# Hand-fetched quarter groups twice as often: a graph layer's row gathers on SyncE and ScalarE

## The reference

```python
h = jnp.maximum(_layernorm(x, axis=-1), 0.0)
cat = jnp.concatenate((h[src], h[dst], edge_attr_128), axis=-1)      # 200000 x 384
msg = jax.nn.relu(cat @ W1 + b1)
aggr = jax.ops.segment_sum(msg, dst, num_segments=12500)
return x + gamma * layernorm(aggr + h) + beta
```

## Time and profile before

| | |
|---|---|
| median of three runs | 2796.62 us (2792.42 to 2845.8) |
| span of the profiled execution, first to last instruction | 1949.5 us |
| the profiled execution's own time | not among the times shown |
| TensorE's mean granted clock | 0.899 |
| HBM read, written | 281.72 MB, 23.64 MB |
| one-row issues of SP and of ACT | 1024 and 1024 |
| POOL's gathers from `table_a` | 1484 |

### The profile page before, as it was taken

How to read it: one execution, slowest core, us unless ns; L and a number is a source line. 1 busy time by engine, 2 the same in 40 slices (tenths; PEclk the granted TensorE clock), 3 DMA queues, 4 the chain that set the end, 5 groups by cost and what they waited for, 6 DMA issues and landing times.

```text
span 1949.5 us, 52908 instructions
## 1 busy us (share of the span) xinstructions
PE 1548.5 (79%) x11881; PEld 1483.7 (76%) x11881; DVE 1256.9 (64%) x3454; ACT 659.4 (34%) x1507; POOL 1463.9 (75%) x1559
## 2 busy tenths in 40 slices
PE   5688788778878787877787788787788888877887
PEld 5678788777777777877777787777777877777786
DVE  7656666667666666666666676666566665656665
ACT  5533333333333333333333333333323232322323
POOL 7777777777777777777777777777777777777776
PEclk9888888989889998998989998999898888888988
DMA  9755656556565655656565565656556565555554
GB/s 261 204 143 144 167 143 166 152 156 166 144 169 145 164 152 155 163 147 169 149 160 153 155 166 144 168 140 168 147 154 163 138 164 148 155 148 153 163 145 106
DMA packets 229468, 306.84 MB, mean 157 GB/s; under 512 B 46461, under 2 KB 141157, under 8 KB 229317
## 3 DMA queue, kind: packets, MB, share of 16 engines
q1 hardware_dynamic: 151858, 192.55, 34.4%
q0 software_dynamic: 49536, 101.55, 21.4%
q10 hardware_dynamic: 27922, 11.43, 2.7%
HBM read 281.72 MB, written 23.64 MB: 157 GB/s over the span
## 4 chain that ended last, share of the span: by engine, by line
issue 22%; DMA 22%; POOL 20%; PE 13%; DVE 10%; DVEq 8%; ACT 2%; ACTq 2%; POOLq 1%; SPq 0%
DMA a_rows<-table_a,picks 20%; POOL a_rows L613 19%; DVEq L1398 5%; DVE onehot_cols L1367 3%; PE ps_pre L769 3%; PE ps_pre L770 3%; PE ps_sum L781 2%; DVE msg L1387 2%; PE ps_edge L756 2%; PE ps_fin L781 1%; DVE aggr L1408 1%; ACTq L1027 1%; DMA table_a<-a_out 1%; DVEq L1383 1%; PE ps_sum L788 1%
## 5 line engine op out<-in xcount | busy, mean ns | idle before, releaser
L613 POOL DMA_INDIRECT a_rows<-table_a,picks x1484 | 1401.8, 945 | 452.4 <-issue 400.3
L769 PE MATMUL ps_pre<-w_c,edge_cols 128*128 128x128 f32 x3128 | 671.5, 300 | 29.5 <-issue 29.2
L770 PE MATMUL ps_pre<-b_win,onehot_cols 128*128 128x128 f32 x3128 | 663.2, 297 | 0.0
L995 ACT ACTIVATE msg<-msg 128x512 f32<-128x512 f32 x390 | 245.7, 630 | 951.9 <-DVE msg L1387 893.1
L769 PEld LDWEIGHTS ps_pre<-w_c,edge_cols 128*128 128x128 f32 x3128 | 537.1, 215 | 38.6 <-issue 37.0
L1387 DVE TENSOR_TENSOR msg<-ps_pre,a_rows 128x512 f32<-128x512 f32 x374 | 257.0, 687 | 433.8 <-DMA a_rows<-table_a,picks 339.4
L770 PEld LDWEIGHTS ps_pre<-b_win,onehot_cols 128*128 128x128 f32 x3128 | 534.7, 214 | 0.0
L1367 DVE SCALAR_TENSOR_TENSOR onehot_cols<-space,base_all,ps_hot 64x512 f32<-64x512 int32 x391 | 438.3, 1121 | 0.6 <-DMA space<-in_dst 0.6
L781 PE MATMUL ps_sum<-onehot,msg 128*128 128x64 f32 x1560 | 214.6, 283 | 105.2 <-ACT e_rows L1013 71.3
L781 PEld LDWEIGHTS ps_sum<-onehot,msg 128*128 128x128 f32 x1560 | 200.5, 201 | 123.4 <-ACT e_rows L1013 82.2
L991 ACT ACTIVATE edge_cols<-ps_edge 128x512 f32<-128x512 f32 x391 | 228.4, 584 | 136.8 <-PE ps_edge L756 115.7
(11 more groups left out here) (137 smaller groups left out, 1073.8 us busy)
## 6 DMA issues: line engine op xcount, KB each, us to landing
edges<-in_edge_attr SPq DMA_DIRECT2D x195, 512.0 KB
space<-in_dst SPq DMA_DIRECT2D x195, 256.0 KB
a_rows<-table_a,picks POOLq DMA_INDIRECT x1484
hand_rows<-table_a SPq DMA_DIRECT2D x1024, 0.5 KB
hand_rows<-table_a ACTq DMA_DIRECT2D x1024, 0.5 KB
b_win<-table_b SPq DMA_DIRECT2D x391, 32.0 KB
table_b<-b_rows ACTq DMA_DIRECT2D x96, 64.0 KB
out<-out_rows SPq DMA_DIRECT2D x96, 64.0 KB
```

Of the source, the lines that this page charges most:

```text
L613: pool.indirect_dma_start(a_rows[:, u, k, :], None, table_a[:, :], bass.IndirectOffsetOnAxis(ap=picks[:, u, k:k + 1], axis=0),).then_inc(s ...
L769: pe.matmul(to, edge_cols[:, u % 2, k * P:(k + 1) * P], w_c[:, :], start=True, stop=False)
L770: mm = pe.matmul(to, onehot_cols[:, u % 2, k * P:(k + 1) * P], b_win[:, u, :], start=False, stop=True)
L995: act.activation(msg[:, u % 2, :, :], msg[:, u % 2, :, :], ACT.Relu).then_inc(s_msg, 1)
```

## The change

PERIOD goes from 6 to 3: a quarter group in each third round is fetched by hand, 32 lists (HANDS) for 16, so POOL gathers three quarters for group 0 in each third round. Of each list's 128 rows SP now issues 80 (ten batches of eight), ACT 48 (twelve slots of four). In a turn of three rounds SP sends a batch after each window of the first two (four a round) and after the first two windows of the third; ACT sends a slot in each group of all three. The lists run one round ahead of their use: the round of use is the first of the turn for the next list. In the first two rounds SP's ten batches are packed closer and ACT sends eights. `hand_rows` gets a second buffer (each with its semaphore), used in turn, and a list waits for the use of the list two before. `hand_picks` is laid out in places of 16 numbers (64 bytes) of which the first eight are used. The loops of POOL, ACT and DVE are cut at the rounds with a hand-fetched quarter; SP's loop still has six rounds a turn, its last turn stands outside the loop.

```diff
-PERIOD = 6
+PERIOD = 3
 BATCH = 8
+PLACE = 16
-ACT_ROWS = 64
+ACT_ROWS = 48
...
-        hand_picks = sb("hand_picks", [HANDS, P], I32)
-        hand_rows = sb("hand_rows", [P, 1, H])
+        hand_picks = sb("hand_picks", [HANDS, P // BATCH, PLACE], I32)
+        hand_rows = sb("hand_rows", [P, 2, H])
...
         def hand_numbers(t, first, n):
+            batch, at = first // BATCH, first % BATCH
             if isinstance(t, int):
-                return hand_picks[t:t + 1, first:first + n]
-            return bass.at_runtime_partition(hand_picks[0:1, first:first + n], t)
+                return hand_picks[t:t + 1, batch, at:at + n]
+            return bass.at_runtime_partition(hand_picks[0:1, batch, at:at + n], t)
+
+        def hand_slots(s, j):
+            t = s * 2 + (0 if j < 2 else 1 if j < EARLY - 1 else 2)
+            third = j + 1 if j < 2 else j - 2 if j < EARLY - 1 else 0
+            return t, (j + 1) // PERIOD % 2, third
+
+        def hands_used(t):
+            return ((t - 2) * PERIOD + PERIOD - 1) * UNROLL + 1
...
                 def fetch(t, par, batch):
-                    if batch == 0 and past(t, 1):
-                        sp.wait_ge(s_z, ((t - 1) * PERIOD + PERIOD - 1) * UNROLL + 1)
+                    if batch == 0 and past(t, 2):
+                        sp.wait_ge(s_z, hands_used(t))
                         sp.sem_inc(s_gate_sp, 1)
                     numbers = numbers_of(mybir.EngineType.SP, t, batch * BATCH, BATCH)
-                    for n in range(BATCH):
-                        sp.dma_start(hand_row(batch * BATCH + n, par), row_at(numbers[n])
+                    for p in range(BATCH):
+                        sp.dma_start(hand_row(batch * BATCH + p, par), row_at(numbers[p])
                                      ).then_inc(s_hand_rows[par], 16)
...
                         window(i, u, base[u])
-                        if t is not None and (j, u) in SP_SLOTS:
-                            fetch(t, par, SP_SLOTS.index((j, u)))
+                        if hands is not None:
+                            t, par, batches = hands
+                            for batch in batches[u]:
+                                fetch(t, par, batch)
...
-                SP_SLOTS = [(j, u) for j in range(1, PERIOD - 1) for u in (1, 3)]
+                SP_BATCHES = [[[0], [1], [2], [3]], [[4], [5], [6], [7]], [[8], [9], [], []]]
+                SP_FIRST = [[[0], [1], [2], [3]], [[4], [5, 6], [7], [8, 9]]]
...
+                def hand_round(i, groups):
+                    for u in range(groups):
+                        step(i, u, HAND_K if u == 0 else SUB)
...
-                        if t is not None and j * UNROLL + u < len(ACT_SLOTS) and ACT_SLOTS[j * UNROLL + u]:
-                            fetch(t, par, j * UNROLL + u)
+                        if hands is not None:
+                            t, par, first, n = hands
+                            if first + u * n < ACT_ROWS:
+                                fetch(t, par, first + u * n, n)
...
-                ACT_SLOTS = [0] * UNROLL + [4] * (ACT_ROWS // 4)
+                SLOT, FIRST_SLOT = BATCH // 2, BATCH
...
-            dve.tensor_scalar(hand_picks[:, :], hand_ids[:, :, HAND_K], float(ROW_BYTES), None, ALU.mult
-                              ).then_inc(s_hand_picks, 1)
+            dve.tensor_scalar(hand_picks[:, :, 0:BATCH],
+                              hand_ids[:, :, HAND_K].rearrange("t (b e) -> t b e", e=BATCH), float(ROW_BYTES), None,
+                              ALU.mult).then_inc(s_hand_picks, 1)
...
-                        dve.wait_ge(s_hand_rows[0], handed * (P * 16))
-                        dve.tensor_tensor(msg[:, u % 2, HAND_K, :], ps_pre[u % 2][:, HAND_K * H:], hand_rows[:, 0, :],
+                        dve.wait_ge(s_hand_rows[par], handed * (P * 16))
+                        dve.tensor_tensor(msg[:, u % 2, HAND_K, :], ps_pre[u % 2][:, HAND_K * H:], hand_rows[:, par, :],
                                           ALU.add).then_inc(s_z, 1)
```

More of the change, by code:

```diff
@@ L535, in _ @@
                 rounds(0)
-                with sp.Fori(1, EARLY_GROUPS) as s:
+                with sp.Fori(1, EARLY_GROUPS - 1) as s:
                     rounds(s)
+                rounds(EARLY_GROUPS - 1)
                 round_(ROUNDS - 2)
@@ L623, in rounds @@
                                 step(s * EARLY + j, u)
[L624 to L625 removed]
+                        hand_round(s * EARLY + (n + 1) * PERIOD - 1, UNROLL - n)
                 for i in range(EARLY):
[L628 to L630 removed]
+                    if i % PERIOD == PERIOD - 1:
+                        hand_round(i, UNROLL - i // PERIOD)
+                    else:
+                        for u in range(UNROLL):
+                            step(i, u)
                 with pool.Fori(1, EARLY_GROUPS) as s:
@@ L1017, in store_early, with fetch, round_ @@
                     act.dma_start(table_early[bass.ds(r * P, P), :], e_rows[:, :]).then_inc(s_e_stored, 16)
-                def fetch(t, par, slot):
-                    if slot == UNROLL and past(t, 1):
-                        act.wait_ge(s_z, ((t - 1) * PERIOD + PERIOD - 1) * UNROLL + 1)
+                def fetch(t, par, first, n):
+                    if first == 0 and past(t, 2):
+                        act.wait_ge(s_z, hands_used(t))
                         act.sem_inc(s_gate_act, 1)
[L1024 to L1029, removed]
+                    numbers = numbers_of(mybir.EngineType.Activation, t, SP_ROWS + first, n)
+                    for p in range(n):
+                        act.dma_start(hand_row(SP_ROWS + first + p, par), row_at(numbers[p])
+                                      ).then_inc(s_hand_rows[par], 16)
+                def round_(i, groups=UNROLL, early=False, early_before=False, hands=None):
                     last = groups < UNROLL
@@ L1431, in clear, with round_ @@
                     dve.tensor_copy(aggr[:, bass.ds((j + AHEAD) * P, P)], ps_zero.to_broadcast([P, P]))
-                def round_(i, turn, groups=UNROLL, early=False, loaded=None):
+                def round_(i, turn, groups=UNROLL, early=False, loaded=None, handed=None, par=None):
                     last = groups < UNROLL
@@ new lines, in _ @@
+                for j in range(PERIOD - 1):
+                    round_(j, turns(0, j), early=True)
+                first_hand(0, True)
+                with dve.Fori(PERIOD, EARLY - 1) as j:
+                    round_(j, turns(0, j), early=True)
+                second_hand(0, True)
+                half = EARLY_ROWS // EARLY
+                with dve.Fori(1, half) as s:
+                    rounds(s, True)
+                for j in range(PERIOD - 1):
+                    round_(half * EARLY + j, turns(half, j), early=True)
@@ L1499, in _ @@
+                first_hand(half, True)
+                for j in range(PERIOD, EARLY - 1):
+                    round_(half * EARLY + j, turns(half, j), early=j < EARLY_REST)
+                second_hand(half, False)
                 with dve.Fori(half + 1, EARLY_GROUPS) as s:
                     rounds(s, False)
-                round_(ROUNDS - 2, ROUNDS - 1 - EARLY_GROUPS)
-                round_(ROUNDS - 1, ROUNDS - EARLY_GROUPS, LEFT)
+                round_(ROUNDS - 2, turns(EARLY_GROUPS, 0))
```

88 lines of the change are left out of this document (50 added, 38 removed).

## The result

The changed kernel takes 3143.64 us (median of four runs, 3135.31 to 3149.0), the kernel before 2799.97 (median of four, 2792.42 to 2845.8): a ratio of 1.121, 95% interval 1.1167 to 1.1252.

The account below looks back on a forecast made before the run. POOL's gathers bound the kernel (113.7 us per six rounds); SP would take over at 121.8. Start 197, turns 1705 and 108, end 44.5 give span 2054, 105 over 1949.5; 2796.62 + 105 = 2901 us, range 2815 to 2955.

Parts of the forecast that it names:

- What bounds the kernel: POOL's stream of gathers sets the pace: 91 at 1.2495 us, 113.7 us in six rounds; 16 fewer save 20.0 us.
- The 847 us: Profile span is 847 us under the runs' median; taken as lying outside the span and unchanged by the change.
- SP's own work: SP's loop, issues and waits' own cost: 78.1 us in six rounds, rising to 121.8 with twenty batches for eight.
- theory A: Posed for the experiments, after the prediction: POOL's gathers slow SP's queue, and the change gives SP more instructions to be slowed.
- The slack: SP's waits, 534.6 us in 15 turns or 35.6 a turn, hid its work and would be used up.
- SP becomes the bound: SP at 121.8 us in six rounds against POOL's 112.5; edges, receivers and windows stand behind slow batches.
- the prediction's list of signs: SP's waits under 100 us, early loads every 121.8 us, POOL idle until DVE's adds, DVE waiting for products, not gathers.
- Order, not place: SP's loads of eight are slow after row issues, not by 64-byte position: six batches at 3.29 us, fourteen at 3.58.
- All of the run is stretched: Rival, 0.07: runs are slower throughout by 1.43, so the 105 us loss becomes 151; 2947 us.
- POOL staying the bound: Rival, 0.08: SP keeps up, a batch costing under 3.06 us, and POOL stays the bound; 2777 us.
- all loads fast: Rival, 0.20: by place, all SP's batches are fast, 117.2 us a turn, +35 us; 2832 us.
- DVE's add of hand rows: Late-rows rival, 0.03: DVE waits some 2 us at each of 32 lists for ACT's last slot; 2841 us.

Follow-up runs that it names:

- shown execution: The profiled execution of the unchanged kernel before, read for the prediction; span 1949.5 us, against a median of 2796.62 us for the runs.
- no_hand: Kernel before with no row fetched, POOL gathering all four quarters of group 0 every round; 2803.25 us, ratio 0.9828.
- before_again: Kernel before, unchanged, profiled once more beside the experiments; 2815.68 us beside 2812.78, span 2799.1 us.
- before_few: Kernel before with only the first quarter of each group gathered by POOL, hand rows still fetched; 1674.42 us.
- few_gathers: Changed kernel with only the first quarter of each group gathered (375 for 1468 gathers), hand rows still issued; 2145.13 us.
- sp_pairs: Changed kernel with SP's rows fetched two to a DMA, 1280 issues fewer; 2865.07 us.
- old_layout: Changed kernel with the row numbers packed as before, 8 numbers a place for 16; 3143.43 us.
- act_rows: Kernel before with all 128 rows of a list issued by ACT, eight a slot, none by SP; 2909.08 us, ratio 1.0237.
- pool_busy: Changed kernel with only each group's first quarter gathered, POOL doing an iota and a memset for each gather left out; 2147.83 us.

## Why the prediction was wrong, point by point

*What bounds the kernel: wrong for the timed runs.* POOL's 113.7 us a turn is what the shown execution shows. In the timed ones POOL waits 844.6 us for DVE, the turn is 163.0, and SP's 144.6 and POOL's 113.7 both fall short of it. With POOL waiting so much, taking 16 gathers off it need not give the 20 us; no_hand, with 16 gathers more and no row by hand, took 1.7% less than before (1.4 to 2.1%).

*The 847 us: the step that failed.* "I take these 847 us as what lies outside the span and unchanged." They lie inside: before_again's span is 849.6 us longer than the shown one, 740 in 15 turns of 163.0 for 113.7, 99 ahead of the first early load, 11 at the end. In a turn SP's own work is 66.5 us longer and its waits 17 shorter, and before_few shows that this goes with the gathers. The sentence should have stopped the working: a profile whose span is 30% under every timed run cannot carry a sum for those runs unless something outside the span is shown, and nothing was.

*SP's own work: the increment right, the base wrong.* 42.4 + 0.5 + 0.8 = 43.7 us a turn were forecast; without most gathers SP's own work is 122.0 (121.8 forecast) against 80.2, +41.8; in the timed kernels 182.4 against 144.6, +37.8. But it starts from 144.6, not 78.1. By few_gathers and before_few the gathers left out there add 64.4 us a turn before (144.6 - 80.2) and 60.4 after (182.4 - 122.0). So they slow SP about as much in either kernel: the second half of theory A, that the change gives them more to slow, is not borne out, and sp_pairs says the same.

*The slack: half of what was read.* 35.6 us of waits a turn were to hide most of the new work; in the timed runs 18.4 were there, and 17.3 were used. So a turn grew by 20.5 us, not by 121.8 - 113.7 = 8.1. This is how the 847 us reached the forecast: as a fixed part they would drop out of the difference, but the slack was read in an execution that the timed runs were not like. Of the 236 us that the forecast fell short, 200 lie in the 15 turns, 27 in the start (33.3 later for 6) and 9 in the end, which did not get shorter. Why the start is so late was not followed.

*SP becomes the bound, with edges, receivers and windows late: right.* SP waits 1.1 us a turn, PE waits 533.8 us for edges, DVE 316.1 for receivers, POOL 1140.4 for DVE. Of the prediction's list of signs two did not come so: the early loads come every 183.5 us and not every 121.8, and DVE's add (line 1426) waits 209.7 us for TensorE's products but 392.9 for a releaser that the trace cannot name, so whether it still waits for gathers stays open.

*Order, not place: right*, by both traces and by old_layout.

*Rivals.* "All of the run is stretched" put the 847 us at the right place, but a common factor isn't what happens: POOL's gathers take 947 ns, 945 in the shown execution, before_few shows SP's work at its normal price, and 2947 was 197 too low: a factor on the 105 us keeps the slack of the shown execution. POOL staying the bound and all loads fast didn't occur; DVE's add of hand rows (line 1433) shows no wait in after. ACT's new slots were put at nothing for hidden; act_rows shows that rows on ACT are not free either (2.4% slower with all 128 rows of a list on ACT and none on SP), but what after's own ACT slots cost was not measured by themselves.

## What to carry to other kernels

Before summing against a profile, set its span beside the timed runs: where they differ by a third, the waits and the slack read from it belong to another execution, and the difference has to be found first. Work put on an issuing queue costs what that queue's waits in the timed runs don't cover, so the waits have to be read from an execution like them. Where indirect gathers of GpSimd run back to back beside a busy SyncE, try a short pause between them: here an iota of 0.48 us behind each, 670 us of added work, made the kernel before 11% faster.

## What the runs showed of the hardware that was not expected

In every profile here with gathers back to back but that of the earlier trace rows, these indirect gathers of POOL hold up SP's queue, and ACT's a little: in after SP's rate falls from 5.1 instructions in 1.25 us beside the first gather to 1.3 beside the eighth, register moves included. An iota of 0.48 us behind each, which spaces the gathers at 1.59 us in place of 1.25, gives most of SP's lost time back. POOL's other work made no difference (pool_busy, 2148 us beside 2145), nor did half the rows a gather (rows64, 3216 beside 3144).

The execution of the earlier trace rows is the exception that no run explains: its 1484 gathers follow each other at 1.25 us throughout, and no row move of SP took over 37 ns. So gathers back to back are not enough by themselves to slow SP. Something else, not found, decides it, and none of the later profiles came out like that one. Open too is what inside the chip is shared, and how much of the wait that PE, DVE and ACT show beside gathers is theirs and how much comes through SP.

A load of eight numbers into registers took SP 0.54 us behind a load of bases and 0.92 behind issues of rows (few_gathers: medians of 95 and 225 loads), a load of four 0.32 and 0.58 (before_few: medians of 34 and 64).
